# Two attention layers in one engine block, meeting at the safety flag instead of at a barrier

## The reference

```
h = relu(layernorm(x))
q, k, v = h @ Wq.T + bq, h @ Wk.T + bk, h @ Wv.T + bv
att = softmax(where(adj > 0, q @ k.T / sqrt(128), -9e15)) @ v
x = x + elu(att)                                        # first layer

node = relu(layernorm(x))
h = node @ W
s1, s2 = h @ a[:128, 0], h @ a[128:, 0]
e = where(adj > 0, leaky_relu(s1[:, None] + s2[None, :], 0.01), -9e15)
x = x + h + softmax(e, axis=1) @ node                   # second layer
```

## Time and profile before

| | |
|---|---|
| median of three executions | 744.18 us |
| the profiled execution, its device time | 744.26 us |
| its span, first to last instruction | 742.4 us |
| TensorE busy | 713.7 us, 96% of the span |
| VectorE, ScalarE, GpSimd busy | 76%, 73%, 61% |
| granted TensorE clock, mean | 0.988 of full |

### The profile page before, as it was taken

The page is one execution under the profiler, slowest core; times in us unless marked ns, Lnnn a source line. Parts: engine busy times, 40 slices in busy tenths (PEclk is TensorE's granted clock), DMA queues, the critical chain, the costliest instruction groups (busy, mean ns, idle before and its releaser), DMA issues. The chain is left out here.

```text
span 742.4 us, 18373 instructions
## 1 busy us (share of the span) xinstructions
PE 713.7 (96%) x6269; PEld 604.4 (81%) x6269; DVE 564.3 (76%) x1207; ACT 540.9 (73%) x1091; POOL 454.5 (61%) x388
## 2 busy tenths in 40 slices
PE   7998999999999999999999999977999999999997
PEld 5667888888888888888888878866888888888885
DVE  6967778787887878878788787797978467577572
ACT  4745867778778787787777877897697797797810
POOL 6778799999999999999999998692000000000000
PEclk9999999999999999999999999998999999999999
DMA  7279999998898978979889773973334353442200
GB/s 241 87 226 304 244 281 237 262 263 234 282 257 248 265 232 281 256 245 265 235 280 255 247 164 86 180 92 87 78 88 87 73 93 68 92 95 64 41 11 13
DMA packets 192783, 132.51 MB, mean 178 GB/s; under 512 B 173536, under 2 KB 180192, under 8 KB 184544
## 3 DMA queue, kind: packets, MB, share of 16 engines
q1 hardware_dynamic: 192000, 131.63, 66.4%
q10 hardware_dynamic: 576, 0.26, 0.1%
q0 software_dynamic: 160, 0.00, 0.0%
HBM read 71.04 MB, written 18.89 MB: 121 GB/s over the span
## 5 line engine op out<-in xcount | busy, mean ns | idle before, releaser
L802 ACT ACTIVATE scores<-scores,neg_max 128x1024 f32<-128x1024 f32 x128 | 146.0, 1142 | 48.2 <-DVE neg_max L937 48.2
L950 DVE TENSOR_TENSOR low<-scores 128x1024 bf16<-128x1024 f32 x96 | 135.5, 1412 | 38.4 <-ACT scores L802 38.4
L1219 PE MATMUL spare<-v_parts,hiT 128*128 128x256 bf16 x768 | 161.7, 274 | 0.0
L931 DVE CUSTOM_DVE_ANT_0 scores<-ps_s,mask_both 128x1024 f32<-128x1024 f32 x128 | 155.9, 1218 | 0.4 <-POOL mask_both L365 0.4
L365 POOL TENSOR_SCALAR mask_both<-mask_bytes 128x2048 bf16<-128x2048 uint8 x64 | 151.8, 2372 | 5.4 <-POOL mask_bytes L360 0.4
L360 POOL TENSOR_SCALAR mask_bytes<-adj_both 128x2048 uint8<-128x2048 int32 x64 | 149.8, 2359 | 3.8 <-DMA adj_both<-in_adj 2.9
L1215 PE MATMUL spare<-v_parts,lowT 128*128 128x128 bf16 x768 | 144.8, 220 | 3.4 <-DMA lowT<-low 3.4
L816 ACT ACTIVATE hiT<-spare 128x512 bf16<-128x512 bf16 (+1 forms) x128 | 102.4, 801 | 35.0 <-PE spare L1189 32.5
L1678 PE MATMUL ps_x<-q_parts,over_k 128*128 128x258 bf16 x1024 | 117.7, 276 | 3.9 <-issue 3.9
L1678 PEld LDWEIGHTS ps_x<-q_parts,over_k 128*128 128x128 fp8e4 x1024 | 100.3, 99 | 19.8 <-issue 4.1
L1154 PE MATMUL ps_s<-k_hi,q_strip 128*128 128x512 f32 x256 | 112.4, 439 | 2.2 <-PEq L83 1.9
(11 more groups left out here) (181 smaller groups left out, 1297.9 us busy)
## 6 DMA issues: line engine op xcount, KB each, us to landing
adj_both<-in_adj SPq DMA_DIRECT2D x64, 1024.0 KB, 5.3
mask_bytes_dram<-mask_bytes SPq DMA_DIRECT2D x32, 512.0 KB, 2.8
x_sb<-in_x SPq DMA_DIRECT2D x8, 256.0 KB, 7.6
out<-res SPq DMA_DIRECT2D x32, 64.0 KB, 1.5
lowT<-low SPq DMA_TRANSPOSE x96, 4.8
mask_both<-s_row_dram SPq DMA_DIRECT2D x2, 768.0 KB, 7.1
over_k<-mask_bytes_dram SPq DMA_TRANSPOSE x16, 4.6
scores<-mask_bytes_dram SPq DMA_TRANSPOSE x16, 4.5
```

Source lines behind the costliest of these rows:

```text
L802: nc.scalar.activation(sc, sc, ACT.Exp, bias=neg_max[:, bn:bn + 1], accum_out=row_sum[:, bn, k:k + 1]).then_inc(exp_done, 1)
L931: nc.vector.tensor_tensor_reduce(out=scores[bn % 2][:, part(k)], in0=ps_s[k % 2][:], in1=mask[bn % 2][:, part(k)], scale=1.0, scalar=LOWES ...
L950: nc.vector.tensor_tensor(low[k][:], p, high_half(p), ALU.subtract).then_inc(low_done, 1)
L1219: last = nc.tensor.matmul(ps_a[:], high, v_parts[:, t, :, :], start=first, stop=final)
```

## The change

The second and the third block become one. The first layer's streams become plain functions that are called at the head of each engine's stream, so the barrier between them goes, and with it the order that it gave. In its place:

- DVE signals `flag_ready` when the flag is written, and each engine waits for that ahead of its load in `choose`.
- Each of the 16 splits signals (`high_split`, `low_split`), and PE waits for the split of the chunk ahead of every fourth matmul of strip 0.
- Ahead of strip 1 PE also waits for ACT's copy of the last piece of s1 (`s1_out`).
- On PE `hw_product(5)` is moved ahead of the top value's turn, and 12 unused products of 128x256 are put behind it. `hw_product(6)` comes between the turn and the spreading, `hw_product(7)` behind it, and then 16 more unused products. They write a PSUM bank whose content nobody reads any more.
- DVE no longer waits for its own flag before `cut_upper(0, 0)`.

`ident_half` is kept for the whole kernel, names are changed, and SP waits for two more loads on the `general` path, which isn't run.

```diff
-                    tail.do(nc.vector.tensor_scalar(flag[:], top[:, 1:2], SAFE, None, ALU.is_le))
+                    nc.vector.tensor_scalar(flag[:], top[:, 1:2], SAFE, None, ALU.is_le).then_inc(flag_ready, 1)
...
-                        split_words(pool, c, 0)
+                        split_words(pool, c, 0).then_inc(high_split, 1)
...
-                                split_words(pool, n, 1)
+                                split_words(pool, n, 1).then_inc(low_split, 1)
...
+                    def unused_products(n):
+                        for _ in range(n):
+                            nc.tensor.matmul(turned_x[0][:, 0:2 * D], ident_half[:], ident[:].bitcast(BF16), start=True, stop=True)
+
                     s_products(NP2 - 1)
                     pe.wait_ge(s_out, NP2 - 1)
                     s1_product(1, ps_s3[1])
                     hw_product(4)
+                    hw_product(5)
+                    unused_products(12)
                     pe.wait_ge(top_ready, 1)
                     nc.tensor.transpose(ps_s2[0:2, 0:D], top[:], ident[:])
                     nc.tensor.matmul(ps_s2[:, D:2 * D], ones[:], hT_diag[:], start=True, stop=True).then_inc(top_t, 1)
-                    hw_product(5)
+                    hw_product(6)
                     pe.wait_ge(top_d, 1)
                     nc.tensor.matmul(ps_s2[:, 0:2], ones[0:2, :], top_diag[:], start=True, stop=True).then_inc(top_b, 1)
-                    for c in range(6, NC):
-                        hw_product(c)
+                    hw_product(7)
+                    unused_products(16)
...
                 def choose(eng, fast, general):
+                    eng.wait_ge(flag_ready, 1)
                     way = eng.value_load(flag[0:1, 0:1], min_val=0, max_val=1)
...
                 @block.tensor
                 def _(pe):
+                    first_layer_tensor(pe)
+
                     def fast(pe):
...
                                 wait(pe, sums_out, s - 1)
+                                if isinstance(s, int) and s == 1:
+                                    pe.wait_ge(s1_out, 2)
...
-                                        if isinstance(s, int) and s == 0 and k == 1 and t % 4 == 0 and t // 4 >= LOW_EARLY:
-                                            pe.wait_ge(low_split, t // 4 - LOW_EARLY + 1)
+                                        if isinstance(s, int) and s == 0 and t % 4 == 0:
+                                            pe.wait_ge((high_split, low_split)[k], t // 4 + 1)
```

More of the change, by code:

```diff
@@ L229, in build @@
         ones = sb(whole, "ones", [D, D], F32)
+        ident_half = sb(whole, "ident_half", [D, D], BF16)
         eps = sb(whole, "eps", [D, 1], F32)
@@ L351, in build @@
         with ExitStack() as first:
-            ident_half = sb(first, "ident_half", [D, D], BF16)
             mask_bytes = [sb(first, f"mask_bytes{i}", [D, N], U8) for i in range(2)]
@@ L551, in build @@
             low_weighed, low_by_scalar = sem("low_weighed"), sem("low_weighed_by_scalar")
+            high_split, low_split, flag_ready = sem("high_split"), sem("low_split"), sem("flag_ready")
             EARLY = slice(0, 2)
@@ L1408, in general @@
                     def general(sp):
+                        for words in words_in:
+                            sp.wait_ge(words, 64)
                         for i, cs in enumerate(S1_CHUNKS):
@@ L1547, in general @@
                                 dve.wait_ge(g_spread, c)
-                                last = nc.vector.tensor_copy(s2_row[:, 512 * c - 512:512 * c], ps_t[(c - 1) % 2][:])
+                                last = nc.vector.tensor_copy(s2_row[:, 512 * c - 512:512 * c], ps_g[(c - 1) % 2][:])
                         last.then_inc(g_s2, 1)
@@ L1644, in strip @@
                             act.wait_ge(g_max, s + 1)
-                            nc.scalar.activation(scores, scores, ACT.Exp, bias=neg_max[:, 0:1],
+                            nc.scalar.activation(scores_g, scores_g, ACT.Exp, bias=neg_max[:, 0:1],
                                                  accum_out=row_sum[:, 0, 0:1]).then_inc(g_exp, 1)
@@ L1694, in general @@
                             pe.wait_ge(g_diag, c + 1)
-                            nc.tensor.matmul(ps_t[c % 2][:], ones[:], pT_g[c % 2][:], start=True, stop=True).then_inc(g_spread, 1)
+                            nc.tensor.matmul(ps_g[c % 2][:], ones[:], pT_g[c % 2][:], start=True, stop=True).then_inc(g_spread, 1)
                         pe.wait_ge(g_s2, 1)
@@ L1705, in strip @@
                                         col = 512 * j + D * i
[L1706 removed]
+                                        last = nc.tensor.transpose(ps_g[j % 2][:, D * i:D * i + D], scores_g[:, col:col + D], ident[:])
                                     last.then_inc(g_t, 1)
@@ L1712, in strip @@
                                         t = 4 * (j - 1) + i
-                                        nc.tensor.matmul(ps_a, high_half(words), h_parts[:, t, :, :], start=(t == 0), stop=False)
-                                        last = nc.tensor.matmul(ps_a[:, 0, :], low_half(words), h_parts[:, t, 0, :], start=False,
+                                        nc.tensor.matmul(ps_ga, high_half(words), h_parts[:, t, :, :], start=(t == 0), stop=False)
+                                        last = nc.tensor.matmul(ps_ga[:, 0, :], low_half(words), h_parts[:, t, 0, :], start=False,
                                                                 stop=(t == T - 1))
```

45 lines of the change are left out of this document (21 added, 24 removed).

## The result

The changed kernel took 738.85 us (median of 6, 736.70 to 740.13), the kernel before 744.12 us beside it (median of 6, 742.88 to 747.09): ratio 0.9927, 95% interval 0.9905 to 0.9949. The forecast was 739.7, in a range of 737.0 to 742.4. The profiled execution took 738.41 us, with a span of 736.5. That is the first of three measurements of this kernel; on which chip it was taken isn't on record.

A forecast was written before the change was run, and what follows sets the result against it. PE, busy 96% of the span, was taken as the bound, its strips running without pause from 505.00. Strip 1 would begin at 510.0 instead of 514.6, so 744.26 - 4.6 = 739.7 us; range 737.0 to 742.4.

The forecast's parts named there:

- The barrier and the flag: At the edge, without the barrier and with the flag's load hidden, PE begins strip 0 at 500.75, 4.25 us earlier.
- it can't pass queued work: Rival: the flag's load costs 1.0 us again on DVE and PE; about 740.5, chance 0.12.
- DVE's way to strip 1: DVE's steps from 500.70, slowed beside POOL's splits, make strip 1 ready at 510.0; 6.70 us before.
- the high end: Ahead of strip 1, DVE and POOL take strict turns, ending at 510.1; the low end was 507.4.
- the 2x2 step: An earlier DVE step that took 0.65 us, ending with a POOL split; evidence for strict turns.
- The row of the normalising: A small DVE step ran in 0.19 us beside POOL's normalising; evidence for the low end.
- The rival that DVE is not held up: Small steps pass between splits, strip 1 is ready at 507.4 and begins at 507.9; 737.6, chance 0.22.
- The pause costs no clock: The 1.9 us pause ahead of strip 1 keeps full clock; the rival had it cost 1.7 us, 741.4, chance 0.25.
- The strips behind: Strip 2 ready at 515.6, needed at 517.2; strip 4 ready at 530.8, needed at 531.5; both narrowly hidden.
- The unused products: On PE around the top value's turn, they cost nothing as long as the clock is full.
- my rival: At half clock the unused products hold the flag up 2.0 us and keep PE till 505.1; 745.4, chance 0.06.
- The 2.4 us of half clock: Time the first four strips lost to half clock before; forecast as saved, with strip 0 at full clock.

The follow-up runs named there:

- e1_zeroed_halves: Changed kernel, but POOL writes zeros into the low halves of lower chunks 4 to 7 instead of splitting them; 740.58 us, ratio 0.9965 (chip A).
- e2: Changed kernel without its two groups of unused products (12 and 16); 739.59 us, ratio 0.9951 (chip A).
- e14: e13 without the two groups of unused products; 737.67 us, ratio 0.9935 (chip C).
- e8: Changed kernel, but ACT weighs lower chunks 6 and 7 and DVE takes four more tiles of signs from ACT; 743.83 us, ratio 0.9999 (chip B).
- e4: Changed kernel, but ACT, not DVE, forms the weighted rows of lower chunks 6 and 7 before the flag; 740.13 us, ratio 0.9958 (chip A).
- e13: e12 with ACT weighing lower chunks 6 and 7 and DVE taking four more sign tiles, as in e8; 739.68 us, ratio 0.9960 (chip C).
- e0: The changed kernel measured again, nothing edited; 744.59 us, ratio 1.0008 (chip B).
- e12: Changed kernel, but PE turns s1 of the lower 24 tiles into rows and one transfer replaces six 4-byte-element stores; 739.31 us, ratio 0.9947 (chip C).
- e7: Changed kernel, but PE waits for the split of lower chunk 5 ahead of strip 0; 742.56 us, ratio 0.9975 (chip B).
- e11: The changed kernel once more, as control on chip C; 740.39 us, ratio 0.9972.
- e5_filled_pause: Changed kernel with 12 more unused products between strips 0 and 1; 744.86 us, ratio 1.0009 (chip B).

## Why the prediction was right, and where it was not

**The barrier and the flag: right to a tenth.** Strip 0 stands 9.11 us behind the top value before (505.00 - 495.89) and 4.86 after (499.33 - 494.47): 4.25 us, the number of the forecast. The load at 497.6 is hidden under queued work on all engines, as PE's sequencer at the drain had led me to expect. The rival that it can't pass queued work is out.

**DVE's way to strip 1: right, and the cause is shown.** 9.06 us measured, 9.3 forecast, 6.70 before. The choice for the high end, by the row of the 2x2 step, was the right one: three small steps lose a turn each, one passes freely. e1_zeroed_halves takes the last four splits away and gets 5.8, where a kernel with the splits and the same late start has 8.27. The Trainium skill's rule ("SBUF — State Buffer", Who interferes with whom) agrees here with steps of 1.02, 0.98 and 0.97 us that take 0.19 to 0.23 without a split beside them. The row of the normalising was no guide for a split. The rival that DVE is not held up is out.

**The pause costs no clock: right, but not for the reason given.** 1.64 us ahead of strip 1, 1.65 in e2 and e14 and 1.86 in e8 all have the clock at 1.00 behind them, while the earlier trace rows had it fall behind 1.94 and 1.99. That looks as if the length decided, as the prediction argued. It doesn't alone: in the first layer of e1_zeroed_halves PE stood still for 3.14 us and kept the full clock behind it (the matmul after the pause, then a stretch).

```profile
63.99 0.22 PE L1211 MATMUL spare<-v_parts,lowT 128*128 128x128 bf16 x1 [3.14 <-DMA lowT<-low]
```

```profile
64.00:65.00 1.00, 1.00 (x13) 0.93 (x14) 0.61 (x4) 0.71 (x2) 0.97 (x1) 1.00 1.20 453
```

So the forecast that this pause would cost nothing came true in part by luck.

**The strips behind: right.** Strips 2 and 4 are not late in the changed kernel. They are only just hidden, as e4 (0.69 and 0.40 us) and e13 (0.21) show once strip 1 comes sooner.

**The sum.** Strip 1 comes 508.30 - 494.47 = 13.83 us behind the top value, 514.6 - 495.89 = 18.7 before: 4.9 us, forecast 4.6. From the profiles, 744.26 - 738.41 = 5.85 us: 4.9 at the edge, 1.4 ahead of it that is no doing of the change, and 0.4 lost again in the tail (736.5 - 508.30 = 228.2 against 742.4 - 514.6 = 227.8).

**The unused products: the step that was wrong.** I put them at nothing, "as long as the clock is full", gave their standing in the way a chance of 0.06, and credited them with the full clock across the edge. In eight of the eleven profiles that have the 12 products, `hw_product(4)` and `(5)` ahead of them run wholly or partly at half clock (3.3 to 3.6 us for 16 matmuls in e0, e12 and e13, instead of 1.95), the 12 end late, and the top value is held up by 1.2 to 2.9 us (by 0.75 in e2, with the slow products and no unused ones). In e7, e8 and e11 that is more than the 2.0 us of my rival; what didn't come is its slow products behind the top value, up to 505. The price comes often, and it is paid ahead of the flag, where everything waits. On the other side they save little: without the barrier no wait behind the flag is longer than 1.65 us, with or without them, and the clock stays at 1.00 behind these waits. The 2.4 us of half clock that I had them help to save are saved without them as well, in e2 and e14: they went with the barrier's pause.

**What the prediction didn't have.** PE's pauses with no semaphore at the end of strip 0. No row of the kernel before could show them, since PE was idle at that time. The stores could have been read there: q1 of the kernel before has 44.7% from 490 to 504 with 0.15 MB moved. An engine that is set free earlier can meet what the wait had covered; what it met here is open. Where this decides, on chip B, the forecast of 739.7 would be wrong by 5 us; the range held the first measurement (738.85) and the one on chip C (740.39), and not the one on chip B (744.59). So that the first measurement came within 0.9 us of the forecast is in part luck: the terms at the edge were right, and its profile has neither of the two losses that they leave out.

## What to carry to other kernels

A barrier's price is read at the engine that sets the end, and so is what it hides: list what else is slow while that engine waits (DMA queues of tiny packets, other engines' turns at a port), because it can come into the open once the wait is gone. Work put in only to keep a clock up must stand where nothing waits for it; ahead of the one value for which all engines wait, it can cost more than the clock does. And where executions differ by 1 to 2 us ahead of the place of a change, compare from a common step just ahead of it to a common step behind it; one profile and one chip are too little for a gain of half a per cent.

## What the runs showed of the hardware

- TensorE can stand still for 0.65 to 2.1 us at a time with no wait that the profile shows, in kernels whose other engines go on undisturbed (of the kernels with the stores and without the barrier, in all four profiles of chip B and in one of the five others). In e5_filled_pause no DMA packet is on record as under way during the longest of these pauses.
- The block of TensorE's instructions that comes during the stores of s1 took 1.2 us in the changed kernel's first profile and 3.5 us in e0_changed_again; without those stores 0.9 to 1.1 us. Its time doesn't go with the pauses: 3.4 us in e2 and none, 1.8 us in e5 and the longest.
- Behind six transfers of 4-byte elements, 2 KB each, the first 768 KB broadcast lands in 12.0 us (changed kernel), behind one transfer of 24 rows the two take 5.0 (e12_turned_store). Why is not shown.
- A POOL step that only writes can stretch a DVE step as well: 1.36 us beside POOL's zeros against 0.68 (e1_zeroed_halves).
- A longer pause can keep the clock that a shorter one loses: TensorE stood still for 1.99 us in the kernel before and had half clock behind it, for 3.14 us in e1_zeroed_halves and had full clock.
- The same kernel gained 0.73% in its first measurement (the chip isn't on record), 0.28% on chip C and nothing on chip B, with the kernel before at 742.9 to 744.1 us in each. Each was measured on one occasion, so chip and occasion can't be told apart.
- Two pauses of about 1.1 us each ahead of the last scores were followed by half clock in ten of the fourteen profiles and by full clock in the others, of the same kernel too (changed and e0_changed_again).
